# One product over two rows in place of two over 128: the bias of an output projection

## What is computed

```
h  = layernorm(x)
q, k, v = split(h @ w_qkv); q, k rotated; 16 heads of 16
a  = softmax(q k^T / 4) v                      # 8 x 512 x 256
p  = a @ w_out + b_out                         # the output projection and its bias
x  = x + layernorm(p)
y  = layernorm(x)
moe = top-2 of 16 experts (256 -> 128 -> 256, silu), weights by softmax of the two logits
shared = (silu(y @ sfc1^T) * (y @ sfc2^T)) @ sfc3^T
out = x + layernorm(moe + shared)
```

## Time and profile before

| | |
|---|---|
| runs (3): median, lowest, highest | 917.66, 910.24, 919.96 us |
| the profiled execution: its time, its span | 915.94 us, 914.1 us |
| granted TensorE clock, mean | 0.945 |
| busy share of the span: PE, DVE, ACT, POOL | 85%, 71%, 57%, 41% |

### The profile page before, as it was taken

The page is one execution under the profiler, slowest core; times in us unless marked ns, Lnnn a source line. Parts: engine busy times, 40 slices in busy tenths (PEclk is TensorE's granted clock), DMA queues, the critical chain, the costliest instruction groups (busy, mean ns, idle before and its releaser), DMA issues. The chain is left out here.

```text
span 914.1 us, 14969 instructions
## 1 busy us (share of the span) xinstructions
PE 776.8 (85%) x4690; PEld 479.2 (52%) x4690; DVE 650.4 (71%) x1256; ACT 520.9 (57%) x1047; POOL 372.9 (41%) x442
## 2 busy tenths in 40 slices
PE   4578798998998989989978877999999788888784
PEld 3433343343443433434422336877877688877673
DVE  4488689688697888887878836778765455553775
ACT  1226577676676777766756754343442466665363
POOL 4430171451630814515300001565665076766442
PEclk9869899898998999989989999999999899999998
DMA  8966637727737568367275401354466355555994
GB/s 157 240 127 167 133 74 157 179 83 163 163 103 170 100 145 179 98 160 163 92 148 88 186 1 52 126 163 150 134 189 210 107 168 172 175 164 193 296 164 92
DMA packets 112421, 133.29 MB, mean 146 GB/s; under 512 B 16724, under 2 KB 80726, under 8 KB 112344
## 3 DMA queue, kind: packets, MB, share of 16 engines
q1 hardware_dynamic: 98616, 108.39, 47.5%
q0 software_dynamic: 13248, 23.15, 9.7%
q10 hardware_dynamic: 480, 0.79, 0.6%
HBM read 68.18 MB, written 59.87 MB: 140 GB/s over the span
## 5 line engine op out<-in xcount | busy, mean ns | idle before, releaser
L480 DVE TENSOR_REDUCE negmax<-ring 128x2 f32<-128x1024 f32 x256 | 306.7, 1212 | 90.4 <-PE ring L643 89.7
L430 ACT ACTIVATE probs<-scores 128x512 f32<-128x512 f32 x498 | 273.6, 599 | 117.3 <-PE scores L661 114.4
L661 PE MATMUL scores<-q_st,k_st 64*128 64x512 f32 x498 | 208.0, 477 | 29.2 <-DMA q_st<-max_rows 16.5
L643 PE MATMUL ring<-k_st,q_st 48*128 48x512 f32 x512 | 187.1, 482 | 26.1 <-issue 9.7
L661 PEld LDWEIGHTS scores<-q_st,k_st 64*128 64x128 f32 x498 | 84.3, 194 | 178.8 <-ACT probs L430 103.1
L675 PE MATMUL av<-probs,v_aug 128*32 128x512 f32 x1024 | 145.0, 640 | 6.3 <-ACT probs L430 6.3
L331 POOL CAST part_r<-negmax 128x16 fp32r<-128x16 f32 x32 | 7.6, 238 | 208.7 <-DVE negmax L480 208.7
L643 PEld LDWEIGHTS ring<-k_st,q_st 48*128 48x128 f32 x512 | 73.3, 199 | 36.7 <-issue 23.1
L166 POOL TENSOR_TENSOR scratch<-qk_raw,cos 128x512 f32<-128x512 f32 x29 | 37.1, 1278 | 82.9 <-ACT qk_raw L383 81.8
L1518 POOL DMA_INDIRECT rows_out<-m_y,projected x48 | 47.3, 985 | 48.1 <-ACT m_y L1583 37.7
L1669 DVE TENSOR_TENSOR m_h_lo<-scores,m_h_hi 128x512 fp32r<-128x512 f32 x40 | 27.6, 691 | 52.2 <-ACT m_h_hi L1569 52.0
(11 more groups left out here) (253 smaller groups left out, 1635.3 us busy)
## 6 DMA issues: line engine op xcount, KB each, us to landing
q_st<-rows_in SPq DMA_DIRECT2D x96, 128.0 KB, 4.5
k_st<-rows_in SPq DMA_DIRECT2D x90, 128.0 KB, 5.5
experts<-split SPq DMA_DIRECT2D x8, 1024.0 KB, 6.0
projected<-records SPq DMA_DIRECT2D x48, 129.0 KB, 2.2
split<-O SPq DMA_DIRECT2D x24, 256.0 KB, 3.0
experts<-rows_out SPq DMA_DIRECT2D x10, 512.0 KB, 8.1
m_rows<-records SPq DMA_DIRECT2D x32, 129.0 KB, 2.4
X<-in_x SPq DMA_DIRECT2D x8, 512.0 KB, 5.0
```

The costliest lines, as they stand in the source:

```text
L430: nc.scalar.activation(probs[r // 2 % 2][r % 2][:, a, :], score_of(R)[:, a, :], ACT.Exp, scale=HD ** -0.5).then_inc(exp_done, 1)
L480: nc.vector.tensor_reduce(negmax[Gn % 2][:, t, 2 * p:2 * p + 2], ring[t % 2][:, :, :], AX.X, ALU.max, negate=True).then_inc(max_done, 1)
L643: last = nc.tensor.matmul(half[:, a, :], q[rows, t * P:(t + 1) * P], k[rows, :], start=True, stop=True)
L661: nc.tensor.matmul(score_of(R)[:, a, :], k[rows, kt * P:(kt + 1) * P], q[rows, :], start=True, stop=True).then_inc(sc_ps, 1)
```

## The change

The two bias products of a tile become one. Its stationary operand is two rows of the matrix of ones, its streamed operand the two parts of the bias as two rows of one partition each: ones x high + ones x low. These two rows are loaded by a small transfer of their own (two partitions x 256 elements) behind that of `small`. `ones_r` is filled in the attention in place of `ident_r`, which goes, and the filling in the middle block goes too. The waits on `small_in` and `masks` follow.

```
-    upper_r, ones_r, ident_r = (pairs[:, 4 * N + i * P:4 * N + (i + 1) * P] for i in range(3))
+    upper_r, ones_r = (pairs[:, 4 * N + i * P:4 * N + (i + 1) * P] for i in range(2))
+    bias_parts = pairs[0:2, 5 * N:5 * N + D]
...
-                for j, bias in enumerate(part(small, BIAS, D)):
-                    nc.tensor.matmul(out_ap, ident_r[:, :], bias, start=t % 2 == 0 and j == 0, stop=False, skip_group_check=True)
+                nc.tensor.matmul(out_ap, ones_r[0:2, :], bias_parts, start=t % 2 == 0, stop=False, skip_group_check=True)
...
+        sp.dma_start(bias_parts.rearrange("k (a r) -> k a r", r=P).bitcast(F32),
+                     split.rearrange("c p a k r -> c p k a r")[CHUNKS - 1, 0, :, D // P:2 * D // P]).then_inc(small_in, 16)
...
-            pe.wait_ge(small_in, 16)
+            pe.wait_ge(small_in, 32)
...
-            nc.scalar.copy(ident_r[:, :], ident[:, :]).then_inc(masks, 1)
+            nc.scalar.activation(ones_r[:, :], ident[:, :], ACT.Copy, scale=0.0, bias=1.0).then_inc(masks, 1)
...
-            nc.scalar.activation(ones_r[:, :], upper[:, :], ACT.Copy, scale=0.0, bias=1.0).then_inc(masks, 1)
...
-                    pe.wait_ge(masks, 3)
+                    pe.wait_ge(masks, 2)
```

## The result

In 22 runs of each, the changed kernel took 919.7 us in the median and the kernel before 911.88 (its first three runs had 917.66). The ratio is 1.0075, 95% interval 1.0048 to 1.0101, so the change costs 6.8 us, between 4.4 and 9.2.

The account below looks back on a forecast made before the run. TensorE was taken to bound the kernel, busy 111.49 of 122.20 us, with all eight projections on the path. Batches 2 to 7 (4.6 us), batch 0 (0.5) and batch 1 (0.5) gave +5.6 us: 922 us, range 911 to 928.

Parts of the forecast that it names:

- batches 2 to 7: Projections in the middle block: three tiles of +0.21 us and a first of +0.13 each, 4.6 us for all six.
- batch 0: Projection at the attention's end, taking turns with ScalarE: +0.02 and +0.21 us for a half's two tiles, twice, 0.5 us.
- batch 1: Projection partly at the lower clock: tiles of +0.05, +0.12, +0.12 and +0.21 us, 0.5 us in all.
- Going in: TensorE's stream runs empty at the change from whole-array products to the two-row product: 0.09 us a tile.
- the exposed loading: Loading the two rows of ones, not hidden beside a running product: 0.06 us, between bounds of 0.02 and 0.10.
- A tile in mid-stream: A projection's tile behind another: losses of 0.33 us less the saved product's 0.12, +0.21 us.
- the waits of 0.48 and 0.79 us: TensorE's waits in a middle step for VectorE's `t_lo` and `multiply`; claimed to stay unchanged, absorbing none of the loss.
- The ring through `first_statistics`: Middle step: a later projection delays VectorE's statistics, `low`, the gate and `multiply` equally, so all eight projections count in full.
- Rival (c): Emptied stream drops the granted clock in projections of batches 2 to 7: 20 us, some 937 us in all; chance 0.04.
- Rival (a): Two rows cost no change of rows in TensorE's stream, leaving only the saving of 4.0 us: 911.9 us; chance 0.13.
- (b): The loss exists but TensorE's two waits in a middle step cover the 0.76 us: 915.9 us; chance 0.06.
- The small transfer and the fillings: Bias transfer behind `small` and moved fillings of `ones_r`: claimed to cost nothing, covered by 9 us and over 20.

Follow-up runs that it names:

- the second profile: The changed kernel measured and profiled again with no edit, against the kernel before: 924.07 us against 912.73, ratio 1.0114 (1.0068 to 1.0161).
- the moves alone: The changed kernel with the two bias products of before, `ident_r` filled beside `ones_r`, against the kernel before: 913.91 us against 911.5, ratio 1.0038.
- the two profiles of before: The kernel before, unchanged, profiled at first and once more on another chip, where one run took 959.79 us (951.94 us there as the base).

## Why the prediction was right

It said slower by 5.6 us, forecast 922 us and a change within 1%; measured are +6.8 us (4.4 to 9.2) and 919.7 us. The mechanism was the right one, and two terms were mis-sized, both too small. That the number came so near is in part luck. The terms as the profiles show them, 5.6 for batches 2 to 7, 0.6 for batch 0, 2.6 for batch 1 and 0.7 for the step behind it, make 9.5 us and not 5.6; and the base of the 922 us was 4 to 6 us too high, as the kernel before takes 911.88 in the median of 22 runs.

**The tile.** Going in 0.09: as predicted. The two-row product itself 0.31 in place of my 0.27: the exposed loading is 0.10, the high end of my bounds, not 0.06. The next one's exposed loading 0.10, not 0.09. A tile in mid-stream is +0.25, not +0.21. I had read the loading from four products in a run, where the later ones' loads have cover, and taken the middle of two bounds, of which the lower, 0.02, does not follow from the 0.065 us beside it. A batch is +0.93 in place of +0.76: three tiles in mid-stream are 0.75 of it, and the first tile, which I put at +0.13, is the other 0.18.

On the page "TensorE: Matmul & The Clock Gate", section "LDWEIGHTS (loading the stationary operand)", the Trainium skill has a load take its columns over 1.2 GHz whatever the rows. I had set this aside; where the load is uncovered the 0.10 us behind a change speaks for it, for 2 rows as for 64 and 128. The four loads of 16 rows in 0.35 us still do not fit it.

**The path.** Six batches of +0.93 us appear in full, as the waits of 0.48 and 0.79 us did not shrink. The ring through `first_statistics` is right; for gains it ends after some 0.7 us, where VectorE takes over.

**Batches 0 and 1.** Batch 0 cost 0.6 us (from its first L879 to the L661 behind its last tile 7.58 us, 526.54 to 534.12, in place of 6.95, 526.80 to 533.75), where I had put 0.5. Batch 1 is where the sum failed most. I put it at +0.5 with two tiles at the lower clock. It cost +2.6 us up to the transpose, since all four tiles ran at the lower clock, where one takes 2.09 us (553.66 to 555.75):

```profile
553.66 0.58 PE L879 MATMUL ring<-projected 2*128 2x256 f32 x1
554.17 0.58 PE L733 MATMUL ring<-projected,t_lo 128*128 128x256 f32 x1
...
555.75 0.58 PE L879 MATMUL ring<-projected 2*128 2x256 f32 x1
```

Before had 1.71 for such a tile (551.71 to 553.42, its trace), so a change costs +0.38 a tile there and not my +0.12. Four tiles of 1.71 would have taken 6.4 us from the first L733 on; so, as an estimate, about half of the 2.6 us is the drains at the lower clock (7.7 less 6.4) and half the clock that did not rise (6.4 less 5.1). Rival (c), which I gave 0.04, thus came true in one place of seven, and not in batches 2 to 7, where I had looked for it and where the clock was 1.00. Its sign, a clock below 1.00 between 554 and 676 us, did show, up to 566.80: the clock did not fall because of the drains, it failed to rise. The step behind is longer too, 19.78 us in the second profile against 18.13, 0.7 more than the drains. The spans of the two profiles of the changed kernel, 924.9 and 921.9 us, lie 10.8 and 7.8 us over the 914.1 of before, and the ratio of the second measurement is 6 to 15 us; so such stretches are not equally long in each run, and what they cost on average I can't give closer than the ratios.

**The rest.** Rival (a) fell with the distances around L879, (b) with the unchanged waits. The small transfer and the fillings show no place in the profile, though the moves alone came out at 1.0038.

## What to carry to other kernels

And between chips the same program took 912 and 952 us. Of the 44 us between the two profiles of before, 38 lie in the last block, behind the middle block's last transposes (676 to 914 us, and 682 to 958), with the same 1293 products, at a mean granted clock of 0.94 and 0.89; the later statistics in the middle steps are only some 3 us of it. The cause stays open.
